# Moving the modulation vectors to the end of a pass, the turning of x ahead of the second hidden layer, and the key copy behind the gate sigmoid

## The reference

```python
nx = _layer_norm(x, ln_gamma, ln_beta)
weights = softmax((nx @ Wq) . (ctx @ Wk) * H ** -0.5)          # 77 prototypes for each sequence
evidence = weights @ (ctx @ Wv)
combined = concatenate([nx, evidence, cond], axis=-1)
router_probs = softmax(combined @ router_W + router_b)         # 3 experts
h = silu(combined @ e_w1 + e_b1)                               # 3 x 256 hidden units
routed = sum((h @ e_w2 + e_b2) * router_probs[..., None], axis=-2)
g = sigmoid(silu(combined @ gate_w1 + gate_b1) @ gate_w2 + gate_b2)
x = x + g * (routed @ out_w + out_b)

# what the third and fourth layers need of cond alone
ss = silu(c) @ W_ss + b_ss            # scale and bias of the third layer's two norms
affine = t_emb @ aff_w + aff_b        # gamma and beta of the fourth layer's two norms
```

## Time and profile before

| | |
|---|---|
| median of three runs | 1090.08 us (1088.79 to 1090.18) |
| the profiled execution | 1088.79 us, its span 1087.0 us |
| PE, matmuls | busy 1026.8 us, 94% of the span |
| DVE | busy 780.5 us, 72% |
| ACT | busy 587.6 us, 54% |
| POOL | busy 684.3 us, 63% |
| granted PE clock, mean of the span | 0.975 |
| the routed layer's passes 1 to 8 | from 422.3 to about 597 us of the span |

### The profile page before, as it was taken

The page is one execution under the profiler, slowest core; times in us unless marked ns, Lnnn a source line. Parts: engine busy times, 40 slices in busy tenths (PEclk is TensorE's granted clock), DMA queues, the critical chain, the costliest instruction groups (busy, mean ns, idle before and its releaser), DMA issues.

```text
span 1087.0 us, 28798 instructions
## 1 busy us (share of the span) xinstructions
PE 1026.8 (94%) x11743; PEld 647.2 (60%) x11743; DVE 780.5 (72%) x1949; ACT 587.6 (54%) x825; POOL 684.3 (63%) x784
## 2 busy tenths in 40 slices
PE   5899999999998999999999699999999999999898
PEld 4445555666654776667766545655556566565476
DVE  6778988778884343777777878889888766777321
ACT  1034444566765555455544256665666677766652
POOL 6568988677975332111215589987878766688530
PEclk8699999999999999999999789999999999999999
DMA  5310000000000112000000000000000000000001
GB/s 183 107 39 3 12 21 12 11 22 22 11 22 21 39 30 96 13 6 7 6 7 18 7 13 2 2 2 2 1 2 2 2 2 2 2 2 2 1 36 42
DMA packets 9282, 22.76 MB, mean 21 GB/s; under 512 B 1392, under 2 KB 1648, under 8 KB 8768
## 3 DMA queue, kind: packets, MB, share of 16 engines
q1 hardware_dynamic: 9152, 20.94, 5.7%
HBM read 18.77 MB, written 2.15 MB: 19 GB/s over the span
## 4 chain that ended last, share of the span: by engine, by line
PE 79%; DVE 10%; issue 4%; POOL 4%; ACT 3%; DMA 0%; DVEq 0%; POOLq 0%; ACTq 0%
PE weighed L657 12%; PE scores L630 10%; PE row_scores L599 8%; PE scores L842 6%; PE weighed L680 5%; DVE negmax L1153 4%; PE quads L538 4%; PE scores L556 4%; PE quads L563 3%; PE row_scores L842 3%; PE scores L642 3%; PE quads L549 2%; PE weighed L853 2%; ACT p L1615 2%; PE scores L670 2%
## 5 line engine op out<-in xcount | busy, mean ns | idle before, releaser
L1153 DVE TENSOR_REDUCE negmax<-row_scores 128x8 f32<-128x616 f32 (+1 forms) x312 | 299.3, 959 | 90.6 <-PE row_scores L599 72.8
L1615 ACT ACTIVATE p<-scores 128x1024 f32<-128x1024 f32 (+1 forms) x256 | 247.6, 1018 | 162.4 <-PE scores L642 161.4
L630 PE MATMUL scores<-qblk,work 32*77 32x512 f32 (+1 forms) x1280 | 203.6, 611 | 10.6 <-ACT p L1615 6.9
L1787 POOL TENSOR_TENSOR kblk_r<-work,pack_const 128x308 fp32r<-128x308 f32 (+1 forms) x160 | 133.7, 836 | 80.1 <-PE row_scores L599 60.1
L657 PE MATMUL weighed<-p,v 77*32 77x128 f32 (+1 forms) x5120 | 173.3, 276 | 2.5 <-DVE nat L1178 2.5
L1777 POOL TENSOR_TENSOR qblk<-work,pack_const 128x512 f32<-128x512 f32 x160 | 166.1, 1038 | 0.6 <-PE scores L630 0.6
L599 PE MATMUL row_scores<-kblk_r,qr 32*128 32x308 f32 (+1 forms) x624 | 141.6, 445 | 19.5 <-DVE negmax L1153 18.7
L657 PEld LDWEIGHTS weighed<-p,v 77*32 77x32 f32 (+1 forms) x5120 | 130.2, 109 | 37.9 <-issue 35.1
L599 PEld LDWEIGHTS row_scores<-kblk_r,qr 32*128 32x128 f32 x624 | 61.7, 186 | 120.9 <-issue 84.5
L1824 POOL TENSOR_TENSOR attn<-nat,rden 128x128 f32<-128x128 f32 x160 | 65.7, 411 | 59.2 <-DVE rden L1183 57.6
L1178 DVE STREAM_TRANSPOSE nat<-weighed 128x256 f32<-128x256 f32 x160 | 70.8, 443 | 34.4 <-PE weighed L657 34.0
(11 more groups left out here) (299 smaller groups left out, 1871.7 us busy)
## 6 DMA issues: line engine op xcount, KB each, us to landing
shared<-gates_hbm SPq DMA_DIRECT2D x24, 256.0 KB, 3.1
shared<-in_ctx_tok SPq DMA_DIRECT2D x15, 154.0 KB
pack_w_l<-in_w_l SPq DMA_DIRECT2D x1, 2058.5 KB, 10.1
x<-in_x_tok SPq DMA_DIRECT2D x8, 256.0 KB, 6.1
out_x<-x SPq DMA_DIRECT2D x8, 256.0 KB, 2.0
layers_w<-in_w_l SPq DMA_DIRECT2D x1, 1289.0 KB, 10.0
ctxT<-in_ctxT SPq DMA_DIRECT2D x1, 1232.0 KB, 9.2
layers_w<-in_w_ada SPq DMA_DIRECT2D x1, 582.0 KB, 5.0
```

Source lines behind the costliest of these rows:

```text
L630: mm = e.matmul(scores[0:nk, g, :], k_of[q % 3][at, s * nk:(s + 1) * nk], qblk[n % 2][at, :], start=layer.mask != "qk", stop=False, skip_g ...
L1153: e.tensor_reduce(negmax[q % 2][:, 2 * h:2 * h + 2, s * NJ:(s + 1) * NJ], row_banks(n, h)[:, :, 0:NJ * nk].rearrange("p g (j k) -> p g j k ...
L1615: e.activation(p[n % 2][0:nk, 8 * h:8 * h + 8, :], scores[0:nk, 2 * h:2 * h + 2, :].rearrange("p g (j q) -> p (g j) q", j=NJ), ACT.Exp, bi ...
L1787: e.tensor_tensor(kblk_r[n % 2][:, 0:NJ * nk].rearrange("p (j k) -> p j k", j=NJ), k_of[q % 3][:, s * nk:(s + 1) * nk].unsqueeze(1).to_bro ...
```

## The change

On PE `turn_nx(i)` now stands ahead of `hidden_layer(c, 1)`. `modulation` and `output_biases` move from between the first two hidden layers of a pass to the end of the pass before it, behind `project_keys`. DVE's parts move likewise, behind `gate_sum`. On ACT `take_keys(i + 1)` now comes after `gate_sigmoid(c)`.

```diff
@@ tensor_program, routed()
                     if last:
                         hidden_layer(c, 0)
-                    if 0 <= i - 3 < len(MODS):
-                        modulation(i - 3)
-                    if i == 7:
-                        output_biases()
-                    if last:
-                        hidden_layer(c, 1)
                     if now:
                         if i >= 3:
                             w.wait_ge(mod_done, 2 * min(i - 2, len(MODS)))
                         if i >= 7:
                             w.wait_ge(bias_done, 1)
                         turn_nx(i)
+                    if last:
+                        hidden_layer(c, 1)
                     if old:
                         expert_mix(m, 0)
@@
                         gate_layer(c)
                     if i + 1 < NB:
                         project_keys(i + 1)
+                    if 0 <= i - 2 < len(MODS):
+                        modulation(i - 2)
+                    if i == 6:
+                        output_biases()
@@ scalar_program
-                if i + 1 < NB:
-                    take_keys(i + 1)
                 if last:
                     gate_sigmoid(c)
                 if i == NB:
                     attention(1, -14, -7)
+                if i + 1 < NB:
+                    take_keys(i + 1)
```

## The result

The changed kernel takes 1103.97 us (median of four runs, 1103.26 to 1107.8), the kernel before 1089.43 us (1087.35 to 1090.18). The ratio is 1.0145, with a 95% interval from 1.0126 to 1.0166: slower, by 15.8 us at 1.0145, where 11.1 were worked out. The profiled execution has a span of 1101.4 us against 1087.0, 14.4 us more.

The account below looks back on a forecast made before the run. PE's own queue was taken to bound the routed layer. Terms 9.04 + 2.26 + 0.20 + 0.54 - 0.90 = 11.1 us on 1088.79 gave 1099.9; with the median higher, the forecast was 1100.5 us, range 1097 to 1104.

Parts of the forecast that it names:

- PE sets the stage, and a new wait counts in full: Routed layer: PE, busy 23.00 of 23 us, sets the stage's length, so any wait PE gets adds its full length.
- The wait at the five turns, 2.26 us each: Pass 2 to 3 through 6 to 7: PE waits 2.16 us for ACT's copy of the keys, plus 0.10 restart.
- The turn from pass 6 to 7 with 0.2 us on top, and DVE's waits covered: Late nx adds 0.2 us before pass 7's prototype scores; the first hidden layer, 1.72 us, covers the transposes' wait for `mod_done`.
- The turn from pass 1 to 2, 0.54 us: Without a modulation there, the earlier transposes wait for the copy of the keys: 0.44 + 0.10 = 0.54 us.
- Pass 1 gives back 0.90 us: Pass 1: earlier transposes shorten PE's 0.87 us wait for nx, so PE goes on at 426.36 instead of 427.26.
- The clock stays at 1.00 throughout: Routed layer: PE's granted clock was expected to stay at 1.00 despite the new waits, adding nothing to the sum.
- rival 1: PE's clock falls at each of the five new waits, at least 8.5 us more, 1109 to 1118 us; chance 0.07.
- Part is given back later: Work of DVE or POOL fills the gaps, shortening 600 to 620 by at most 2 to 4 us; chance 0.07.

## Why the prediction was wrong

The prediction gave the sign and the mechanism of the waits. It added 11.1 us and forecast 1100.5 us, with a range to 1104. The median after is 1103.97 us, but with its fourth run the median of the kernel before is down to 1089.43: by the ratio the change adds 1.45%, which on the 1090.08 us that the prediction started from is 1105.9, beyond that range. The step that failed is the clock, which was put at nothing in the sum. In the profiled pair the sum is 11.1 as predicted + 0.5 of waits that were sized too low + 5.0 for three falls of the clock + 0.1 ahead of the stage - 2.3 behind it = 14.4 us. Point by point:

- *PE sets the stage, and a new wait counts in full.* Right: 11.6 us of the stage's added 16.6 are the waits and what hangs on them, by the kernels with 9 and 4 filling matmuls.
- *The wait at the five turns, 2.26 us each.* Right: the profile has 10.2 us of idle time in five, 2.1 us the longest, and the modulation begins 3.56 us after the gate layer, 3.57 in the working. PE's restart cost stands as well: the modulation takes 0.63 us where it took 0.53, and at 490.66 load and matmul begin together again. By the Trainium skill (TensorE: Matmul & The Clock Gate, "Architectural detail") PE can pull weight loads ahead of matmuls in flight; behind these waits the trace doesn't show it.
- *The turn from pass 6 to 7 with 0.2 us on top, and DVE's waits covered.* Right within 0.1: with 9 filling matmuls, between gate layers, passes 3 to 6 are 2.25 to 2.31 us longer than before, and pass 7 is 2.41 us longer (25.43 against 23.02).
- *The turn from pass 1 to 2, 0.54 us.* Right: pass 2 is 0.49 us longer (22.84 against 22.35 us between the gate layers of passes 1 and 2).
- *Pass 1 gives back 0.90 us.* Half right. The prototype scores begin 0.92 us sooner (4.09 us after the stage's start, before 5.01), but the gate layer of the pass only 0.44. The rest goes to PE's wait ahead of L888, the transposes of the softmax's weights, which is now 0.65 us and was 0.17. DVE's last step of that softmax, L1290, takes 0.95 us in place of 0.48 before:

```profile
430.71 0.95 DVE L1290 TENSOR_TENSOR p<-p,r_rden 128x308 f32<-128x308 f32 x1
...
431.71 0.66 PE L888 MATMUL scores<-pack_const,p 128*77 128x128 f32 x4 [0.65 <-DVE p L1290]
```

  POOL's subtraction L1889 (430.28 for 1.04 us) now runs when it begins, as in all traces of kernels that turn x early in pass 1, which all have 0.95 to 0.96 us there. In the three that turn it late, and in every later pass, it begins after that subtraction has ended or nearly so, and it takes 0.48. Whether POOL is the cause was not tried. I had followed the gain to PE's next instruction and not to its next wait. This is the half us by which the waits' sum, 11.6, is above mine, 11.1.
- *The clock stays at 1.00 throughout.* Wrong, and this is the step that failed: the sum put the clock at nothing, and the fall of rival 1, to which I gave 0.07, happened at three of the five turns, 5.0 us. The rival was priced for all five. One or two falls I had only as a widening of the range, from 1102.9 to 1104, which is 1.1 us and less than the 1.7 of a single one. The falls of before stood behind idle times of 2.99 and 1.23 us, and 2.16 lies between. I had counted two in these rows, but the mean of 0.77 over 600 to 620 has a further one in it, behind 2.38 us of idle time at 617.01. The reason I gave against it, that matmuls of the whole array stand on both sides, does not hold: it fell in just this stretch. The trace of before had no idle time of that length in so dense a stretch, and where a trace doesn't show a thing its price was to be bounded from both sides, 0 to 8.5 us here, so the range should have gone to 1109 at least. That three of the five fell, and not one or five, could not be had from the rows; the traces since have three or four in one execution each.
- *Part is given back later.* Only 2.3 us in the profiled pair, 1.7 of it a fall of the clock that did not come again at the end. No run ties that to the change: the fall behind that wait stands in 6 of the 13 traces, the one with the keys copied first among them, and not in the one with them copied late alone.

The Trainium skill (TensorE: Matmul & The Clock Gate, "HAM oscillation — how this bites in real kernels") has waits of PE between its bursts bring the clock down, each time. Here waits of 2.0 to 2.1 us did so in a stage in which PE is busy for 179.42 of 190.53 us, but only at some of them.

## What to carry to other kernels

A copy frees a shared PSUM bank here. Moving away the matmuls that covered it cost 0.8 us for each turn, putting two instructions of the copying engine ahead of it 0.6, and both together 2.3, before the clock: look at what stands between the issue and the wait on both engines, and at both edits together. When a change makes a saturated PE wait about 2 us, add the clock to the sum: in this stage 1.65 us for each wait at which it falls, for none to all of them. And when a stage is the question, compare the stage between two landmarks of the trace, which repeated within 0.2 us at the same number of falls, instead of whole times that scatter by several us.

## What the runs showed of the hardware

PE's clock fell to 1.2 GHz behind 16 of 25 waits of 2.0 to 2.1 us (five kernels, one execution each) in a stage of dense float32 matmuls, for 3.4 us each time, and not behind ten waits of 1.1 to 1.2 us nor ten of 0.3 to 0.6 us. Elsewhere in the same traces, among narrow matmuls, it fell behind 11 of 26 waits of 1.23 us. Which waits it fell at differed from trace to trace, for identical instructions too; what decides it is open. It fell after PE had begun to work again: in the turn shown above PE resumes at 490.66 and is at half speed from about 491.8 on, so dense matmuls pay for it and not the idle time. Filling 0.9 of the 2.1 us with matmuls that nobody uses was enough to keep it up at ten waits of ten in two kernels, and made the changed kernel's stage 5.0 us shorter.
